# First pass: the exponential unit's relu and exp two and one steps sooner on ScalarE. Fourth pass: the chain of row lengths behind the next sums on VectorE

## The reference

```python
def _gat_layer(x, src, dst, W, a_src, a_dst, b, n, h, c):
    feat = (x @ W).reshape(n, h, c)
    e = al_s[src] + al_d[dst]
    e = jnp.where(e > 0, e, NEG_SLOPE * e)
    m = jax.ops.segment_max(e, dst, num_segments=n)
    ee = jnp.exp(e - m[dst])
    s = jax.ops.segment_sum(ee, dst, num_segments=n)
    alpha = ee / (s[dst] + 1e-16)
    out = jax.ops.segment_sum(alpha[:, :, None] * feat[src], dst, num_segments=n)
    return out.reshape(n, h * c) + b
...
h = _gat_layer(h, src, dst, W1, a_src1, a_dst1, b1, N, H1, C1)
h = jax.nn.elu(h)
out = _gat_layer(h, src, dst, W2, a_src2, a_dst2, b2, N, H2, C2)
...
# layer 2, after its own attention over the edges
h_combined = h + agg
un_c = jnp.maximum(jnp.linalg.norm(h_combined, axis=-1, keepdims=True), 1e-15)
h_poincare = jnp.tanh(un_c) * h_combined / un_c
norms = jnp.linalg.norm(h_poincare, axis=1, keepdims=True)
return jnp.where(norms > MAX_NORM, h_poincare * (MAX_NORM / (norms + 1e-08)), h_poincare)
```

## Time and profile before

| | us |
|---|---|
| median of three runs | 5120.69 |
| lowest, highest | 5118.16, 5121.72 |
| the profiled execution | 5117.03 |
| its span | 5115.2 |
| busy: TensorE | 4351.1 (85%) |
| busy: VectorE | 4034.4 (79%) |
| busy: POOL | 3123.2 (61%) |
| busy: ScalarE | 2974.8 (58%) |

### The profile page before, as it was taken

The page is one execution under the profiler, slowest core; times in us unless marked ns, Lnnn a source line. Parts: engine busy times, 40 slices in busy tenths (PEclk is TensorE's granted clock), DMA queues, the critical chain, the costliest instruction groups (busy, mean ns, idle before and its releaser), DMA issues. The chain is left out here.

```text
span 5115.2 us, 74853 instructions
## 1 busy us (share of the span) xinstructions
PE 4351.1 (85%) x20185; PEld 3272.2 (64%) x20185; DVE 4034.4 (79%) x13139; ACT 2974.8 (58%) x7633; POOL 3123.2 (61%) x2813
## 2 busy tenths in 40 slices
PE   3999999999958888857888799999867749988887
PEld 2888888888836666645666466666544427765555
DVE  5899999999968788759999388888767769955554
ACT  2999999999934444424555377777645534521111
POOL 3766666666446666537777665555554436647777
PEclk9999999999978999978999899999977769999898
DMA  4888888888854444338898456656468866644443
GB/s 136 296 311 312 309 311 308 310 309 310 302 178 125 133 135 134 117 94 282 300 301 283 154 179 188 189 184 184 146 213 268 267 197 201 208 140 136 148 157 127
DMA packets 652112, 1097.58 MB, mean 215 GB/s; under 512 B 85506, under 2 KB 472458, under 8 KB 651573
## 3 DMA queue, kind: packets, MB, share of 16 engines
q1 hardware_dynamic: 532418, 838.42, 48.0%
q0 software_dynamic: 119168, 253.97, 16.7%
q10 hardware_dynamic: 112, 0.40, 0.0%
HBM read 524.78 MB, written 575.95 MB: 215 GB/s over the span
## 5 line engine op out<-in xcount | busy, mean ns | idle before, releaser
L855 PE MATMUL mm<-w,tt 128*128 128x264 f32 x3136 | 732.5, 387 | 2.6 <-ACT tt L899 2.6
L1424 POOL DMA_INDIRECT got<-F,index x392 | 529.7, 1351 | 264.0 <-PE acc L1607 158.9
L855 PEld LDWEIGHTS mm<-w,tt 128*128 128x128 f32 x3136 | 582.3, 191 | 93.0 <-ACT tt L899 2.8
L1603 PE MATMUL acc<-got,sel 128*128 128x260 f32 (+1 forms) x1176 | 437.7, 460 | 108.3 <-DVE sel L1578 100.1
L1616 ACT ACTIVATE rows<-acc 128x260 f32<-128x260 f32 (+1 forms) x588 | 226.8, 386 | 497.3 <-PE acc L1607 497.1
L821 POOL DMA_INDIRECT place<-PLACE,place_ix x392 | 413.2, 1054 | 119.5 <-issue 119.5
L2761 DVE SCALAR_TENSOR_TENSOR agg<-mask,agg,acc 128x128 f32<-128x128 f32 x784 | 247.8, 344 | 254.9 <-PE acc L2748 140.9
L793 POOL DMA_INDIRECT xd<-in_x_dram,index x196 | 224.9, 1148 | 316.8 <-DMA XD<-xd 285.0
L855 PE MATMUL mm<-wl,tt 128*128 128x264 f32 x1568 | 413.1, 386 | 0.6 <-ACT tt L899 0.6
L1607 PE MATMUL acc<-rows,carry 128*128 128x260 f32 (+1 forms) x1008 | 358.0, 440 | 47.5 <-ACT rows L1616 44.1
L1294 PE MATMUL kv<-wkv,ht 128*128 128x512 f32 x784 | 372.7, 598 | 0.1
(11 more groups left out here) (414 smaller groups left out, 12951.8 us busy)
## 6 DMA issues: line engine op xcount, KB each, us to landing
F<-f1o SPq DMA_DIRECT2D x97, 528.0 KB
F<-f2o SPq DMA_DIRECT2D x97, 528.0 KB
HL<-ho SPq DMA_DIRECT2D x97, 528.0 KB
xin<-in_x_dram SPq DMA_DIRECT2D x97, 512.0 KB, 5.7
H<-h SPq DMA_DIRECT2D x97, 512.0 KB, 3.2
X<-x3o SPq DMA_DIRECT2D x97, 512.0 KB, 3.3
out_dram<-oo SPq DMA_DIRECT2D x97, 512.0 KB
drow<-DSTF SPq DMA_DIRECT2D x84, 448.0 KB
```

The costliest lines, as they stand in the source:

```text
L855: last = nc.tensor.matmul(mm[PAIR[stage, q]][:, r, 0:F2W], lhs[:, q, 2 * r + k, :], w[:, k, :], start=(k == 0), stop=(k == KB - 1))
L1424: nc.gpsimd.indirect_dma_start(out=buf[:, n % SLOTS, t, :], out_offset=None, in_=table, in_offset=bass.IndirectOffsetOnAxis(ap=index[:, n ...
L1603: nc.tensor.matmul(acc, self.sel[:, s, t, :], self.got[:, n % SLOTS, t, 0:w], start=True, stop=False)
```

## The change

In the first pass ScalarE's relu moves from step 6 of its loop to step 4, behind the exponential of the scores, and its exp from step 6 to step 5. In the fourth pass VectorE's lengths of c move behind the block of x (`den`, `hc`), and ScalarE's tanh moves from step 3 to step 5. No instruction is added, removed or resized.

```diff
@@ first pass, ScalarE
                             if within(a) and t == 4:
                                 ph.exponents(act, a)
-                            if within(x) and t == 6:
+                            if within(x) and t == 4:
                                 hold(act, d["x"], x + 1, None)
                                 hold(act, d["g"], x, None)
                                 nc.scalar.activation(zm[:, :, :], o[:, x % SLOTS, :, :], ACT.Relu, scale=-1.0)\
                                     .then_inc(d["neg"], 1)
+                            if within(x) and t == 5:
                                 hold(act, d["neg"], x + 1, None)
                                 nc.scalar.activation(zm[:, :, :], zm[:, :, :], ACT.Exp, scale=-1.0)\
                                     .then_inc(d["exp"], 1)
@@ fourth pass, VectorE
                         if within(a):
                             ph.segment_most(dve, link, a)
-                        if within(c):
-                            hold(dve, d["sq"], c + 1, None)
-                            link(V.tensor_scalar(var[:, :], n2[:, c % 2, :], 1e-30, None, ALU.max))
-                            take(rsqrt(nc, link, rt[:, :], var[:, :], ra[:, :], h=gb[:, :]))
-                            V.tensor_tensor(unc[:, :], var[:, :], rt[:, :], ALU.mult).then_inc(d["unc"], 1)
                         if within(x):
...
                             hold(dve, d["hc"], x + 1, None)
                             dve.sem_inc(d["used"], 1)
+                        if within(c):
+                            hold(dve, d["sq"], c + 1, None)
+                            link(V.tensor_scalar(var[:, :], n2[:, c % 2, :], 1e-30, None, ALU.max))
+                            take(rsqrt(nc, link, rt[:, :], var[:, :], ra[:, :], h=gb[:, :]))
+                            V.tensor_tensor(unc[:, :], var[:, :], rt[:, :], ALU.mult).then_inc(d["unc"], 1)
                         if within(a):
                             ph.differences(dve, link, a)
@@ fourth pass, ScalarE
-                            if within(c) and t == 3:
+                            if within(c) and t == 5:
                                 hold(act, d["unc"], c + 1, None)
                                 nc.scalar.activation(th[:, :], unc[:, :], ACT.Tanh).then_inc(d["tanh"], 1)
```

## The result

The changed kernel takes 5178.1 us (median of 4 runs, 5175.7 to 5180.7), the kernel before in the same comparison 5119.4 (4 runs). The ratio is 1.0118, with a 95% interval from 1.0105 to 1.0131. The forecast was 5164 (+43 on the kernel before, measured +58.7), with a range of 5125 to 5186 and 5148 to 5182 for the case that it took. The profiled execution has a span of 5174.3 against 5115.2, 59.1 more, at a mean clock of 0.921 against 0.927.

The account below looks back on a forecast made before the run. It took the shortest closed chain of waits between groups of seven tiles, not engine work, as the bound. First pass +11 and fourth +32 make +43 on 5117.0, 5160, plus 3.7 for the median: 5164 us, range 5125 to 5186.

Parts of the forecast that it names:

- the case that it took: Whole kernel: first pass +11, fourth pass +32, giving 5164 us; chance 0.48, range 5148 to 5182.
- the block from ScalarE's `wt` to `crow`: First pass: small copy, relu, `rows`, `gt`, `put`, exp and handover to `crow` sum to 4.76 us a group.
- 25 steps of 25.50: First pass: closed chain of 25.50 us a group, 637.5 in all; with the first step 660.0 against 643.1, +16.9.
- would have ended its work some 2 us sooner and then waits for `sel`: First pass: TensorE's 2.84 us stall goes, and the chain through `crow` is what comes late next.
- The drain: End of the first pass: the last exp is done sooner, -6 us, bounds between nothing and 8 gained.
- a step of 16.83: Fourth pass: 25 steps of 16.83 us make 420.8 against 388.5, +32.
- The 6.16 behind the sixth `rows`: Fourth pass: from the sixth tile's `rows` through tanh to TensorE's next first matmul takes 6.16 us.
- the 10.67 to it: Fourth pass: TensorE's first matmul to the sixth `rows`, 10.67 us, mean of five groups after one long idle time.
- ScalarE's squares no longer end it: Fourth pass: the squares stop closing the chain, being done about when the first tile needs them.
- Clock as now: Rival: clock unchanged, fourth-pass step of 16.06, +11 + 13, 5145 us; chance 0.23.
- Full clock: Rival: fourth pass at full clock, step of 13.8, 44 us back in the pass, 5088 us; chance 0.07.
- The first pass gains: Rival: `crow` isn't held by the seventh `rows`, first pass -34, with +32 in the fourth 5119 us; chance 0.05.

Follow-up runs that it names:

- the kernel with the filled waits: First pass's part of the change alone, plus four unread 128x248 matmuls per group at TensorE's two waits: 5122.4 us against 5115.2 before, ratio 1.0008.
- the six matmuls: Fourth pass's part of the change alone, plus six unread 128x256 matmuls at the end of each group: 5080.6 us, ratio 0.9926 to the kernel before.

## Why the forecast was right, and where its terms were off

The direction and the chains held in both passes. The time is 14 us above the forecast, and the change costs 16 us more than forecast (58.7 against 43): 9 of it in the first pass and 3 in the fourth.

- **First pass, the chain.** `crow` to `o<-zm,o` 4.02 without a wait, the block from ScalarE's `wt` to `crow` 4.72 (forecast 4.76), the wait of `crow` for `rows` mostly 3.1 to 4.2, at the ends 1.6 and 5.7 (forecast about 3), TensorE waiting for `sel`: all as said. The step is 25.43 where nothing else intervenes (forecast 25.50), and with TensorE held at the upper clock the 26 steps measure 658.6 (forecast 660.0). This is shown by the kernel with the filled waits.
- **First pass, the term that was mis-sized.** "25 steps of 25.50" gave +16.9, and the 26 steps measure +29.5. The failed step is the sentence that TensorE "would have ended its work some 2 us sooner and then waits for `sel`". It treated TensorE as out of the chain once its 2.84 stall had gone. It also waits for `hot_hi` and `edges`, it comes out of these waits at the low clock in 15 of the 24 groups that have them, and by ScalarE's order its late product, `put` of the third tile, stands ahead of `wt`. These steps are 0.6 or 2.0 longer than 25.5: 12 x 0.6 + 3 x 2.0 = 13.2, less 10 x 0.07 for the others, is 12.5 of the 12.6 that were missing. The sum also set unlike things against each other: 25.50 is a chain without a clock term, and the 643.1 of before had some 10 us of low clock in them (12 steps 0.4 and 3 steps 1.7 above the 24.57 of the others). Taken alike, the chain costs 24 x (25.45 - 24.57) = 21.1 and 4.3 in the first two steps, and the low clock, which is in 15 steps before as after, costs 4.1 more than it did. These make the 29.5.
- **The drain.** Forecast -6, "a microsecond or two more if the next drain gains as well"; it measures -9.5, since both last waits for the exp are shorter (8.84 and 7.75 became 3.99 and 4.66). This hides 3.5 of the 12.6, so that the pass as a whole looks better forecast than its steps were.
- **Fourth pass.** Forecast a step of 16.83, measured 17.07 and 17.2 at first; +32 against +37.3 in the steps, and +35.4 for the pass. The 6.16 behind the sixth `rows` measure 6.18. The mis-sized term is the 10.67 to it, a mean of five groups. The first of them (9.33) started low like the others, for its pair at 3756.81 lasts 1.20 (the earlier trace rows shows half of the pair, 0.77 x1), but had its clock back before the third `rows`; the other four had 10.89 to 11.21, and after the change 24 of 25 groups have 10.87 to 11.10. The forecast's "ScalarE's squares no longer end it" is true of 13 of the 25 steps at most: in the other 12 it was the tanh's chain before too, over the fourth `rows`. The clock was the open term, and of the two readings the one of the earlier trace rows, that a long idle time sends a group off low, was right in all of the 25 groups: the Trainium skill's rule (TensorE: Matmul & The Clock Gate, Part 1), by which the slow state is the default and a gap brings it back, agrees with the 1.20 of each first pair.
- **The rivals.** "Clock as now" is out, at 0.71 against 0.79. "Full clock" is what the six matmuls make of the same order: a step of 13.79 (forecast of that rival 13.8) and 40 us below before. "The first pass gains" is out for the place chosen. With the exp behind the seventh `rows` the pass does gain. The Trainium skill's advice (Perfetto Trace Analysis, Optimizing Scalar/DVE Operations) is to break up instructions of a Scalar that isn't saturated but causes bubbles elsewhere. Nothing was broken up here, two instructions were only moved apart, which is near to it: that agrees with the trace where the exp stands behind the copy that closes the loop (1.11 in place of TensorE's 2.84, 26 us gained with the relu at 3), and not where both stand ahead of it (23 us lost).
- **Open.** The sum leaves 3.2 us in the stages behind the fourth pass and 1.5 in the second and third. Neither was looked into, and they are about the spread of one execution. Why one group in four (tanh at 4) or one in seven (six matmuls) falls back to the low clock isn't settled; the rows show that it does, with equal waits ahead.

## What to carry to other kernels

When a long instruction is moved in an in-order list, add up everything that then stands between the engine's own last input and the instruction that closes the loop. The exp one place later, behind that instruction, turned a loss of 23 us into a gain of 14, and the relu one place earlier made it 26. An engine whose stall you remove is not free afterwards: look at where it will wait next, and at what clock it comes out of that wait, because a late result can stand ahead of the critical instruction in another engine's list. Where the matmul engine idles once per group of some 14 to 17 us, unread matmuls in that idle time are a cheap test of how much of the step is clock, and here a gain by themselves.

## What the hardware showed that was not expected

- In the fourth pass 1.1 us less idle time ahead of a group (2.50 and 1.07 against 3.70 and 0.96) didn't spare it the low clock at its start, but brought the upper one back before the third tile in three groups of four. Those groups take 2.3 to 2.6 us less than the fourth one, more than twice the idle time itself.
- Six unread matmuls of 128x256 a group (2.75 us of TensorE) made the kernel 81 us faster, and four of 128x248 a group in the first pass some 17 to 18 us faster (1.0044 to 1.0008, 17.4 less to the start of the fourth pass in the traces).
- Waits of 1.04 and 1.34 with little work between them left TensorE at the low clock in the first pass in 15 of 24 groups, beside a busy share of 491.60 of 575 us, and in the other 9 they didn't. Before the change, one wait of 2.84 was followed by the low clock in 15 of 24 groups as well, and the mean clock was the same 0.95. Such a step cost 0.4 or 1.7 then, and costs 0.6 or 2.0 now.
